# One step product of weighed halves in the wavefront scan, the logarithm in two pieces, and reworked edges between the stages of a conv-attention kernel

## The chip, the cores and the metric

The kernel runs on one core of one Trainium2 chip. The metric is device time in microseconds for one execution. The median of three runs of the kernel before is 4778.52 us (4757.96 to 4780.98).

## The reference, cut to what matters

The input is 64 images of 32 x 32 cells with 128 channels. Four layers follow one another: a scan, two attention layers, a scan. A scan visits all 1024 cells in a fixed spiral order and rewrites each from itself and its neighbours:

```python
def step(g, inp):                 # ci: the cell; ni, nm, nc: its neighbours, a mask, their number
    local = g[:, ci, :]
    neigh = (g[:, ni, :] * nm[None, :, None]).sum(axis=1) / nc
    u = jnp.concatenate([local, neigh], axis=-1)              # 256 channels
    y_sc = jnp.tanh(u @ w1 + b1) @ w2 + b2                    # 256 hidden values, one scalar a cell
    return (g.at[:, ci, :].set(local + y_sc[:, None] * w_y[None, :]), None)
# attention: q, k of 16 channels, v of 128; all 1024 cells of an image attend to all
attn = jax.nn.softmax(jnp.einsum('bnd,bmd->bnm', q, k), axis=-1)
out = gamma * jnp.einsum('bnm,bmc->bnc', attn, v) + inputs    # gamma in the first layer only
```

Everything is float32.

## The kernel before

**Scan.** Channels lie on the 128 partitions. Cells that don't depend on each other form a level; there are 122 levels with 16 cells at first and 1 at the end (509 cells stand in levels 0 to 35). A level's work is done for 32 images at once in two streams, A and B, up to level 63 (`JOIN` is 64), and from there for all 64 images in one stream. So an operand has 32 x 16 = 512 columns at level 0 and 32 x 11 = 352 at level 35. A product of the 256 hidden values is made in two halves of 128. For a stream and a level:

- POOL adds the neighbours that are not yet updated (`late_sums`, L562).
- DVE adds updated neighbours of older levels (L686) and those of the level just before (L688, together with `b2 * w_y`). The neighbours of the level just before are at that time without their step, so DVE adds the step of that level to the sums from PSUM when it is there (`add_steps`, L711). `EDGES` scales the sums of border cells (L695).
- PE makes `w1_own` times the cell (`own_products`, L906, 2 products), `w1_sum` times the sum (`near_products`, L916, 2 products); ACT takes the tanh of both halves (`squash`, L842).
- PE makes the step, w2[k] * w_y[c] times the hidden values, as 2 products that add up in PSUM (`steps`, L925). DVE adds it to the cells (`update`, L719).

Each engine works its queue in order. PE's order is, for each level, stream A (steps, own and near products of the next level), then B. DVE's is, for each level and stream: `add_steps` of the next level, `update` of this one, `sums` of the level after the next.

The cells live in `arena`, 512 places for each image, filled and emptied by chunks of levels. `load` (L411) and `store` (L417) move one chunk of one stream, as 4096 pieces of a few cells each; all are issued on SP, whose queue is in order too. `ENDING` is a chunk of 16 cells that are last in their ring; `first_loads` brings the chunks that have no earlier tenant of their places, for A, then for B.

**Attention.** 128 jobs (2 layers x 64 images, group A's 32 images through both layers, then B's). A job has 8 slices s on every engine; in a slice PE makes two key products (L954), a row product (L967), and the mix of probabilities and values: one full float32 product (L983) for the even block, and for the odd block three products of rounded parts (L988, L989, L991). The low part of the odd block is made by POOL (`split_probs`, L571) from what DVE rounded (L786). `row_maximum` (L748, DVE) and `row_sums` (L857, ACT) serve the softmax shift of the next job: POOL turns the sums into logarithms in one piece of 12 small instructions at s = 2 (`log_sums`, L582 to L605), between two `split_probs`. PE transposes the shift at s = 5 (`turn_shift`, L1034). `output` (L805, DVE) adds the mix to the image, SP stores it at s = 2 of the next job and loads a later one at s = 3 (`load_image`, L460), from the DRAM tensors `layer_out`.

**Edges.** The first job's image is loaded (L460) once all chunks of group A have been stored. `prepare_scan` weighs the scan weights on DVE, for the second scan after the first scan. 12 jobs before the end (`EARLY`), SP issues `first_loads` of the second scan for A, and after the last job those for B.

## Time and profile before

| | us |
|---|---|
| median of 3 runs | 4778.52 |
| lowest, highest | 4757.96, 4780.98 |
| the profiled execution | 4771.76 |
| its span, first to last instruction | 4769.6 |

| engine | busy us of the span | share |
|---|---|---|
| PE | 4486.8 | 94% |
| PE weight loads (beside the products) | 2312.6 | 48% |
| DVE | 3579.9 | 75% |
| ACT | 2850.4 | 60% |
| POOL | 2278.8 | 48% |

The profiled execution took 2.2 us more than its span. In the trace the first scan takes the time up to about 793 us, the attention jobs from 816 to 3997 us, the second scan the rest. In the timeline rows below, the first number is the start and the second the time taken by the instructions merged in the row; a count (x4) says how many records that is. A float32 product has two records on PE.

### The profile page before, as it was taken

The page shows a single profiled execution, that of the slowest core. Times are in us where ns is not written, and L with a number is a line of the kernel's source. Part 1 is how long each engine was busy: PE and PEld are TensorE (multiplying, and loading weights), DVE is VectorE, ACT ScalarE, POOL GpSimd, SP SyncE. Part 2 cuts the span into 40 slices and gives each one's busy share as a digit, 9 for nine tenths or more (in the row PEclk, how much of TensorE's full clock was granted, in tenths as well). Part 3 has the DMA queues.
Part 4 walks back from the last instruction along what each step waited for, and adds up shares of the span by engine and source line. Part 5 has one row for each costly group of instructions (what it writes and reads, how often), then busy time and mean ns, then how long its engine had stood idle before and what let it go on. Part 6 is the DMA issues. An engine that isn't in the chain of part 4 may idle for free.

```text
span 4769.6 us, 56934 instructions
## 1 busy us (share of the span) xinstructions
PE 4486.8 (94%) x17064; PEld 2312.6 (48%) x17064; DVE 3579.9 (75%) x6748; ACT 2850.4 (60%) x5225; POOL 2278.8 (48%) x3972
## 2 busy tenths in 40 slices
PE   5999996999999999999999999999999798999997
PEld 2456754444444444444444444444444343446754
DVE  3888876777777777777777777777777574888876
ACT  1223322777777777777777777777777574223322
POOL 3454431455555555555555555555555455454431
PEclk7999998899999999999999999999999899999998
DMA  9569415111111111111111111111111515379625
GB/s 155 54 74 127 91 31 56 48 57 57 57 57 57 52 53 55 57 57 56 57 57 57 53 54 54 55 57 57 57 57 57 108 53 96 36 75 127 86 53 45
DMA packets 496962, 309.85 MB, mean 65 GB/s; under 512 B 443408, under 2 KB 446736, under 8 KB 496656
## 3 DMA queue, kind: packets, MB, share of 16 engines
q1 hardware_dynamic: 496656, 306.21, 32.7%
q8 instruction: 138, 2.26, 0.2%
q14 instruction: 168, 1.38, 0.1%
HBM read 137.34 MB, written 135.27 MB: 57 GB/s over the span
## 4 chain that ended last, share of the span: by engine, by line
PE 69%; POOL 14%; DVE 6%; issue 6%; SPq 2%; DMA 1%; ACT 1%; DVEq 0%; POOLq 0%; ACTq 0%
PE psum L983 14%; PE psum L925 9%; PE psum L916 8%; PE psum L906 8%; PE psum L954 7%; POOL probs_low L571 7%; PE psum L991 4%; PE psum L967 4%; PE psum L989 3%; PE psum L988 3%; PE psum L1024 3%; PE psum L1002 3%; PE psum L1011 3%; SPq L411 1%; DVE shared L711 1%
## 5 line engine op out<-in xcount | busy, mean ns | idle before, releaser
L571 POOL TENSOR_TENSOR probs_low<-shared,probs_high 128x512 fp32r<-128x512 f32 x1024 | 1307.9, 1277 | 1387.9 <-DVE probs_high L786 1387.9
L748 DVE TENSOR_REDUCE top<-psum 128x1 f32<-128x1024 f32 x1024 | 1253.5, 1224 | 596.8 <-PE psum L967 596.6
L852 ACT ACTIVATE shared<-psum 128x512 f32<-128x512 f32 x2048 | 1108.9, 594 | 376.0 <-PE psum L954 375.8
L857 ACT ACTIVATE psum<-psum,top 128x1024 f32<-128x1024 f32 x1024 | 1114.3, 1088 | 311.0 <-DVE top L748 311.0
L983 PE MATMUL psum<-shared 128*128 128x512 f32 x2048 | 1127.4, 632 | 3.3 <-DVE x L805 0.7
L842 ACT ACTIVATE shared<-psum,b_col 128x320 f32<-128x320 f32 (+10 forms) x744 | 413.3, 566 | 1101.5 <-PE psum L916 1086.5
L562 POOL TENSOR_TENSOR shared<-arena 128x32 f32<-128x32 f32 (+6 forms) x1230 | 570.6, 494 | 870.4 <-PE psum L916 802.6
L988 PE MATMUL psum<-probs_high,v_high 128*128 128x512 f32 x1024 | 813.1, 794 | 0.0
L906 PE MATMUL psum<-arena,w_own 128*128 128x320 f32 (+12 forms) x1672 | 543.3, 453 | 42.2 <-DMA arena<-x_cells 38.3
L916 PE MATMUL psum<-shared,w_sum 128*128 128x320 f32 (+10 forms) x1488 | 529.4, 478 | 42.1 <-POOL shared L562 28.4
L786 DVE CAST probs_high<-shared 128x512 fp32r<-128x512 f32 x1024 | 538.8, 526 | 21.3 <-ACT shared L852 21.3
L925 PE MATMUL psum<-shared,w2wy 128*128 128x320 f32 (+10 forms) x1488 | 519.0, 471 | 13.8 <-ACT shared L842 7.1
L954 PE MATMUL psum<-q,k 64*128 64x512 f32 x2048 | 513.4, 497 | 0.3 <-ACT shared L852 0.3
L991 PE MATMUL psum<-probs_low,v_high 128*128 128x512 f32 x1024 | 419.6, 410 | 93.2 <-POOL probs_low L571 93.2
L983 PEld LDWEIGHTS psum<-shared 128*128 128x128 f32 x2048 | 306.3, 189 | 367.2 <-ACT shared L852 202.1
L967 PE MATMUL psum<-k,q 64*128 64x512 f32 x2048 | 411.2, 398 | 11.8 <-ACT psum L857 6.0
L906 PEld LDWEIGHTS psum<-arena,w_own 128*128 128x128 f32 x1672 | 306.6, 191 | 232.2 <-issue 138.9
L711 DVE SCALAR_TENSOR_TENSOR shared<-psum,shared 128x32 f32<-128x32 f32 (+10 forms) x954 | 294.1, 345 | 162.2 <-PE psum L925 152.3
L989 PE MATMUL psum<-probs_high,v_low 128*128 128x512 f32 x1024 | 401.8, 392 | 0.0
L916 PEld LDWEIGHTS psum<-shared,w_sum 128*128 128x128 f32 x1488 | 259.0, 191 | 257.7 <-DVE shared L711 123.5
L688 DVE SCALAR_TENSOR_TENSOR shared<-arena,b2wy,shared 128x256 f32<-128x256 f32 (+15 forms) x530 | 305.0, 576 | 100.9 <-POOL shared L562 82.2
L925 PEld LDWEIGHTS psum<-shared,w2wy 128*128 128x128 f32 x1488 | 264.1, 190 | 227.6 <-issue 103.6
(71 smaller groups left out, 4094.8 us busy)
## 6 DMA issues: line engine op xcount, KB each, us to landing
x<-layer_out SPq DMA_DIRECT2D x128, 512.0 KB, 3.2
layer_out<-x SPq DMA_DIRECT2D x128, 512.0 KB, 2.6
q<-q SPq DMA_DIRECT2D x256, 128.0 KB, 2.3
arena<-x_cells SPq DMA_DIRECT2D x8, 1520.0 KB, 10.4
layer_out<-arena SPq DMA_DIRECT2D x8, 1520.0 KB, 19.3
arena<-layer_out SPq DMA_DIRECT2D x8, 1520.0 KB, 10.7
y_cells<-arena SPq DMA_DIRECT2D x8, 1520.0 KB, 20.4
arena<-x_cells SPq DMA_DIRECT2D x4, 1504.0 KB, 18.8
```

Of the source, the lines that this page charges most:

```text
L571: nc.gpsimd.tensor_tensor(probs_low[n % 2][:], probs[u % PROBS], probs_high[n % 2][:], ALU.subtract).then_inc(probs_split, 1)
L748: nc.vector.reduce_max(top[i % 2][:, m:m + 1], rows_ps[m % 2][:], AX_X, negate=True).then_inc(row_max, 1)
L852: nc.scalar.activation(probs[u % PROBS], keys_ps[u % 2], ACT.Exp).then_inc(probs_ready, 1)
L857: nc.scalar.activation(rows_ps[m % 2][:], rows_ps[m % 2][:], ACT.Exp, bias=top[i % 2][:, m:m + 1], accum_out=total[i % 2][:, m:m + 1]).the ...
L906: nc.tensor.matmul(columns(pre(c, lv, h), c, lv, o, w), w1_own[n][:, tile(h)], arena[:, PICTURES[c], place:place + w], start=(m == 0), sto ...
L916: nc.tensor.matmul(columns(pre(c, lv, h), c, lv), w1_sum[n][:, tile(h)], cells(near[lv % 2], c, lv), start=False, stop=True, skip_group_ch ...
L925: mm = nc.tensor.matmul(columns(step(c, lv), c, lv), w2wy[n][h][:], cells(hidden[h], c, lv), start=(h == 0), stop=(h == HALVES - 1))
L954: nc.tensor.matmul(keys_ps[g], k[i % DEEP][ROW_GROUPS[g], tile(m)], q[i % 3][ROW_GROUPS[g], half(queries_at(g, h))], start=True, stop=True ...
L967: mm = nc.tensor.matmul(rows_ps[m % 2][:, half(g)], q[i % 3][ROW_GROUPS[g], tile(queries_at(g, h) * MT // 2 + r)], k[i % DEEP][ROW_GROUPS[ ...
L983: nc.tensor.matmul(mix_ps, v[i % 2][:, t], probs[u % PROBS], start=(m == 0), stop=False).then_inc(mixed, 1)
L988: nc.tensor.matmul(mix_ps, v_high[i % 2][:, t], probs_high[n % 2][:], start=False, stop=False)
L991: nc.tensor.matmul(mix_ps, v_high[i % 2][:, t], probs_low[n % 2][:], start=False, stop=(m == MT - 1)).then_inc(mixed, 1)
```

## The change

- **Levels 0 to 35** (`WEIGHED` = 36): DVE makes one operand `hidden0 + hidden1 * (w2_small / w2_big)` (`weigh`), and PE one step product with the weights of the first half. For the quotient to be at most 1 in size, the halves of w1, b1 and w2 are exchanged, hidden value by hidden value, so that the larger of the two w2 stands first (`larger_first`, 36 small DVE instructions for each scan).
- In these levels `add_steps` is gone. `update` comes first, and the sums over the level just before read the updated cells. PE's order becomes steps A, near B, own A of the next level, steps B, near A of the next level, own B of the next level; DVE's update A, new sums A, weigh B, old sums A of the level after, and the same for B.
- **Logarithm**: the polynomial is rearranged to 12 instructions in two pieces of 6, at s = 2 and s = 3, with one `split_probs` between them.
- **Chunks**: 14 instead of 13; the first are smaller (levels 0 to 1, 2 to 5, 6 to 7: 32, 64 and 31 cells), and the ending chunk takes in levels from 114 on (28 cells instead of 16). The last other chunk ends with level 113. The first loads are ordered by need: four chunks of A, four of B, the other four of A, of B.
- **Scan weights** are loaded on ACT's queue, and `prepare_scan(1)` with its `larger_first` is done by DVE in the midst of the first scan, at level 20.
- **Scan to attention**: the first 4 images are loaded except for their last 66 cells when the chunk before those is stored; ACT copies the 66 cells from `arena`.
- **Attention to scan**: no block of loads 12 jobs before the end. After each job of the second layer two loads put that image's first 511 cells of the second scan into `arena` (`refill`); ACT copies those of the very last image.

The diff, cut to its core:

```diff
-WINDOW = 5 * CHUNK - 16
+TAIL = 114
+WINDOW = 452
...
-    first = [0, 2]
-    for lv in range(2, LEVELS):
+    first = [0, 2, 6, 8]
+    for lv in range(8, TAIL):
...
+        def load_first_images():
+            for k in range(ENDING - 1):
+                sp.wait_ge(stored[A][k], 16)
+            sp.wait_ge(scan_weights_ready, 2 * (2 + HALVES))
+            for i in range(DEEP):
+                sp.dma_start(x[i][:, 0:OPEN], inner[0][i, :, 0:OPEN]).then_inc(x_in[i], 16)
+        def refill(i):
+            if is_job(i) and job_layer(i) == LAYERS - 1 and i < JOBS - 1:
+                g, b = i // (LAYERS * IMAGES), job_image(i)
+                sp.wait_ge(out_stored[i % DEEP], 16 * (i // DEEP + 1))
+                first = PLACES[0]
+                sp.dma_start(arena[:, b, first:first + KEPT], inner[LAYERS][b, :, 0:KEPT]).then_inc(refilled[g], 16)
+                sp.dma_start(arena[:, b, chunk_places_of(ENDING)], inner[LAYERS][b, :, chunk_cells(ENDING)]
+                             ).then_inc(refilled[g], 16)
...
-            load_scan_weights(0)
-            first_loads(0, A)
-            load_scan_weights(1)
-            first_loads(0, B)
+            for part in (FIRST_LOADS[:4], FIRST_LOADS[4:]):
+                for g in (A, B):
+                    for k in part:
+                        load(0, g, k)
...
                     if s == 6:
                         place_shift(j + 1)
+                        refill(j - 1)
...
-                if j == EARLY:
-                    first_loads(1, A)
...
-            first_loads(1, B)
...
             # log_sums(i), at s = 2
             nc.gpsimd.tensor_tensor(ratio[:], shrink[i % 2][:], total[i % 2][:], ALU.mult)
             nc.gpsimd.tensor_scalar(excess[:], ratio[:], -1.0, None, ALU.add)
+            nc.gpsimd.tensor_tensor(log_sum[:], top[i % 2][:], guess[i % 2][:], ALU.subtract)
             nc.gpsimd.tensor_tensor(square[:], excess[:], excess[:], ALU.mult)
+            nc.gpsimd.tensor_scalar(slope[:], excess[:], -0.25, 1.0 / 3.0, ALU.mult, ALU.add)
+            nc.gpsimd.tensor_tensor(slope[:], slope[:], excess[:], ALU.mult)
+        def shift_values(i):     # at s = 3
+            nc.gpsimd.tensor_scalar(slope[:], slope[:], -0.5, None, ALU.add)
+            nc.gpsimd.tensor_tensor(log_sum[:], log_sum[:], excess[:], ALU.subtract)
+            nc.gpsimd.tensor_tensor(slope[:], slope[:], square[:], ALU.mult)
+            nc.gpsimd.tensor_tensor(ratio[:], log_sum[:], slope[:], ALU.subtract)
             nc.gpsimd.tensor_copy(high, ratio[:])
             nc.gpsimd.tensor_tensor(low, ratio[:], high, ALU.subtract)
...
+        def weigh(n, c, lv):
+            dve.wait_ge(tanh_ready[c], levels_done(n, c, lv) * HALVES)
+            nc.vector.scalar_tensor_tensor(cells(hidden[0], c, lv), cells(hidden[1], c, lv), w2_ratio[n][:],
+                                           cells(hidden[0], c, lv), ALU.mult, ALU.add).then_inc(weighed[c], 1)
...
+            for lv in range(WEIGHED):
+                for c in (A, B):
+                    update(n, c, lv)
+                    new_sums(n, c, lv + 1)
+                    if c == A:
+                        weigh(n, B, lv)
+                    elif lv + 1 < WEIGHED:
+                        weigh(n, A, lv + 1)
+                    if lv + 2 <= WEIGHED:
+                        old_sums(n, c, lv + 2)
+                    else:
+                        sums(n, c, lv + 2)
+                if (n, lv) == (0, 20):
+                    prepare_scan(1)
...
         prepare_heads()
-        prepare_scan(1)
...
+        act.wait_ge(updated[BOTH], len(SPAN[BOTH]))
+        fill_first_images()      # 4 x 2 copies arena -> x
...
+        fill_last_picture()      # 2 copies x -> arena, after the last job
...
+            if lv < WEIGHED:
+                pe.wait_ge(weighed[c], n * WEIGHED + lv + 1)
+                nc.tensor.matmul(columns(step(c, lv), c, lv), w2wy[n][0][:], cells(hidden[0], c, lv),
+                                 start=True, stop=True).then_inc(step_ready[c], 1)
+                return
...
+            for lv in range(WEIGHED):
+                steps(n, A, lv)
+                near_products(n, B, lv)
+                own_products(n, A, lv + 1)
+                steps(n, B, lv)
+                near_products(n, A, lv + 1)
+                own_products(n, B, lv + 1)
```

## Rows read from the trace of the kernel before

**Rows 1.** Busy by stretch: PE, PEld, DVE, ACT, POOL; granted clock, DMA share, GB/s

```profile
66.00:395.00 329.00, 328.73 (x872) 159.84 (x873) 268.64 (x738) 90.49 (x140) 164.29 (x390) 0.99 0.62 78
820.00:3700.00 2880.00, 2778.10 (x11373) 1358.66 (x11373) 2188.89 (x2939) 2236.78 (x4113) 1503.98 (x2348) 0.99 0.17 55
```

**Rows 2.** Waits, 820 to 3990 us: total us, times, longest us

```profile
PE psum L991 <- POOL probs_low L571: 93.2, 127, 0.9
...
PE psum L1002 <- DMA x<-layer_out: 25.5, 1, 25.5
```

**Rows 3.** Timeline of PE and ACT about level 34, 352 columns

```profile
380.76 1.35 PE L916 MATMUL psum<-shared,w_sum 128*128 128x352 f32 x4
...
381.55 1.15 ACT L842 ACTIVATE shared<-psum,b_col 128x352 f32<-128x352 f32 x2 [2.51 <-PE psum L916]
...
381.94 1.35 PE L925 MATMUL psum<-shared,w2wy 128*128 128x352 f32 x4
```

**Rows 4.** Groups by form, 66 to 395 us: busy us, mean ns of one

```profile
L842 ACT ACTIVATE shared<-psum,b_col 128x512 f32<-128x512 f32 x30 | 20.6, 688 | 94.9 <-PE psum L916 94.9
...
L688 DVE SCALAR_TENSOR_TENSOR shared<-arena,b2wy,shared 128x352 f32<-128x352 f32 x13 | 7.7, 595 | 0.5
L688 DVE SCALAR_TENSOR_TENSOR shared<-arena,b2wy,shared 128x512 f32<-128x512 f32 x10 | 7.5, 752 | 0.4
...
L842 ACT ACTIVATE shared<-psum,b_col 128x352 f32<-128x352 f32 x10 | 5.5, 555 | 12.5 <-PE psum L916 12.3
```

**Rows 5.** DVE's group of added steps, 66 to 395 us

```profile
L711 DVE SCALAR_TENSOR_TENSOR shared<-psum,shared 128x32 f32<-128x32 f32 (+14 forms) x206 | 74.8, 395 | 40.3 <-PE psum L925 37.8
```

**Rows 6.** Timeline of one job about the logarithm

```profile
2013.39 0.20 POOL L582 TENSOR_TENSOR ratio<-shrink,total 128x8 f32<-128x8 f32 x1
...
2015.19 0.47 DVE L786 CAST probs_high<-shared 128x512 fp32r<-128x512 f32 x1
...
2016.78 1.28 POOL L571 TENSOR_TENSOR probs_low<-shared,probs_high 128x512 fp32r<-128x512 f32 x1
...
2018.11 0.50 PE L991 MATMUL psum<-probs_low,v_high 128*128 128x512 f32 x1 [0.53 <-POOL probs_low L571]
...
2019.20 0.23 PE L1034 MATMUL psum<-ident_r,shift 128*16 128x128 f32 x1
```

**Rows 7.** Timeline of the start; SPq is SP issuing DMAs

```profile
4.56 30.08 SPq L411 DMA_DIRECT2D arena<-x_cells  x7
...
43.97 31.33 SPq L411 DMA_DIRECT2D arena<-x_cells  x7
...
61.25 1.64 POOL L562 TENSOR_TENSOR shared<-arena 128x32 f32<-128x32 f32 x3 [35.96 <-DMA arena<-x_cells]
...
66.27 3.78 PE L916 MATMUL psum<-shared,w_sum 128*128 128x512 f32 x4 [8.47 <-POOL shared L562]
```

**Rows 8.** Timeline from the first scan to the first job

```profile
792.83 0.34 DVE L719 SCALAR_TENSOR_TENSOR arena<-psum,b2wy,arena 128x64 f32<-128x64 f32 x1 [2.27 <-PE psum L925]
...
795.64 0.29 DVE L626 TENSOR_SCALAR w_sum<-w_sum 128x256 f32<-128x256 f32 x1
...
816.11 1.97 PE L1002 MATMUL psum<-x,wk_rows 128*64 128x512 f32 x4 [23.31 <-DMA x<-layer_out]
```

**Rows 9.** SP's queue 12 jobs before the end

```profile
3711.21 28.57 SPq L411 DMA_DIRECT2D arena<-layer_out  x7
```

**Rows 10.** Timeline from the last job to the second scan

```profile
3996.63 1.66 POOL L562 TENSOR_TENSOR shared<-arena 128x32 f32<-128x32 f32 x3 [0.63 <-PE psum L991]
...
3998.36 3.25 POOL L562 TENSOR_TENSOR shared<-shared,arena 128x32 f32<-128x32 f32 x4
...
4019.42 3.78 PE L916 MATMUL psum<-shared,w_sum 128*128 128x512 f32 x4 [9.11 <-POOL shared L562]
```

**Rows 11.** Timeline of the end: SP's last stores, DVE's last update

```profile
4744.47 19.69 SPq L417 DMA_DIRECT2D y_cells<-arena  x4
...
4746.56 0.33 DVE L719 SCALAR_TENSOR_TENSOR arena<-psum,b2wy,arena 128x64 f32<-128x64 f32 x1 [2.12 <-PE psum L925]
```

More of the change, by code:

```diff
@@ L243, in turn_count @@
 def turn_count(n, c, lv):
[L245 removed]
+    per = [len(SUMS_OLD[v]) + len(SUMS_NEW[v]) + len(EDGES[v]) + (step_turns(c, v) if v > WEIGHED else 0)
+           for v in SPAN[c]]
     return n * sum(per) + sum(per[:lv - SPAN[c].start])
@@ L272, in first_chunks @@
     return [k for k in range(NC) if min(first_use[chunk_cells(k)]) == lv]
+FIRST_LOADS = sorted((k for k in range(NC) if not earlier_tenants(k)),
+                     key=lambda k: (min(FIRST_READ[chunk_cells(k)]), -chunk_size(k) if k else -CELLS))
+KEPT = sum(chunk_size(k) for k in FIRST_LOADS if k != ENDING)
+OPEN = STARTS[CHUNKS[ENDING - 1]]
 def is_job(i):
@@ L490, in place_shift @@
                                  shift_row[i % 2][:, cells_of]).then_inc(shift_placed[i % 2], 16)
-        def first_loads(n, g):
-            for k in (0, ENDING, *range(1, ENDING)):
-                if not earlier_tenants(k):
-                    load(n, g, k)
         def follow(n):
@@ L677, in sums, with new_sums @@
                         dve.wait_ge(updated[e], levels_done(n, e, lv - 2))
-            done = 0
-            for o, w, s0, s1 in (*SUMS_OLD[lv], *SUMS_NEW[lv]):
+            for m, (o, w, s0, s1) in enumerate(SUMS_OLD[lv]):
+                out = near[lv % 2][:, PICTURES[c], o:o + w]
+                if s0 is None and m > 0:
+                    dve.wait_ge(near_turn[c], turn_count(n, c, lv) + m)
+                in0 = out if s0 is None else arena[:, PICTURES[c], s0:s0 + w]
+                nc.vector.tensor_tensor(out, in0, arena[:, PICTURES[c], s1:s1 + w], ALU.add
+                                        ).then_inc(near_turn[c], 1)
+        def new_sums(n, c, lv):
+            if lv <= WEIGHED:
+                dve.wait_ge(updated[c], levels_done(n, c, lv - 1))
+            turn = turn_count(n, c, lv)
+            done = len(SUMS_OLD[lv])
+            for o, w, s0, s1 in SUMS_NEW[lv]:
                 out = near[lv % 2][:, PICTURES[c], o:o + w]
@@ L723, in scan @@
         def scan(n):
+            weigh(n, A, 0)
             for c in (A, B):
-                sums(n, c, 1)
-            for lv in range(JOIN - 1):
+                old_sums(n, c, 1)
+            for lv in range(WEIGHED):
[8 more added lines that the diff above has]
+                        old_sums(n, c, lv + 2)
+                    else:
+                        sums(n, c, lv + 2)
+                if (n, lv) == (0, 20):
+                    prepare_scan(1)
+            for lv in range(WEIGHED, JOIN - 1):
                 for c in (A, B):
@@ new lines, in load_weight_rows, with fill_first_images @@
+        def load_weight_rows(n):
+            act.dma_start(x[DEEP - 1][:, n * HID:(n + 1) * HID], scan_weights[n][2].rearrange("(a c) -> a c", a=1).to_broadcast([P, HID])
+                          ).then_inc(scan_weights_in[n], 16)
+        def fill_first_images():
+            for i in range(DEEP):
+                for k in (ENDING - 1, ENDING):
+                    nc.scalar.activation(x[i][:, chunk_cells(k)], arena[:, i, chunk_places_of(k)], ACT.Copy
+                                         ).then_inc(x_tail, 1)
@@ L883, in _ @@
+        with nc.allow_non_contiguous_dma(reason="rows to all partitions"):
+            load_scan_weights(0)
+            load_weight_rows(0)
+            load_scan_weights(1)
+            load_weight_rows(1)
+        act.wait_ge(scan_weights_in[0], 16 * 9)
         for lv in range(LEVELS):
```

182 lines of the change are left out of this document (132 added, 50 removed).

## The prediction

> **What bounds the kernel now.** I read the busy time by stretch first. Levels 0 to 35 of the first scan lie between 66 and 395 us, and there PE is busy 328.73 of 329 us at a clock of 0.99, while DVE has 268.64 and POOL 164.29 [rows 1]. The reader should see that PE alone sets this stage: a product less is time less, as long as nothing else comes up to it. In the attention jobs PE has 2778.10 of 2880 us, ACT 2236.78, DVE 2188.89. The waits say what the rest is: 93.2 us before L991, once in each job (127 times), for POOL's low parts, and one wait of 25.5 us for an image [rows 2]. The timelines of the start, of the two changes of stage and of the end then show stretches in which PE has nothing to do because data or sums are late [rows 7 to 11].
>
> **Step products of levels 0 to 35.** Two step products are issued 381.94 - 380.76 = 1.18 us after two near products of 352 columns began [rows 3], so a product of that width takes h = 0.59 us, and one of 512 columns 0.86 us. A half cycle (one stream, one level) has 6 products now: 5.15 us at 512 columns, 3.54 us at 352. It keeps 5: 4.29 and 2.95 us. The mean level has 509 / 36 = 14.1 cells, 452 columns, h = 0.76 us. There are 36 levels x 2 streams x 2 scans = 144 half cycles, so the bound of the gain is 144 x 0.76 = 109 us.
>
> Against it stands a longer chain. From a stream's steps A to the steps B that follow, PE makes steps A and near B, then ACT the second tanh of B, then DVE weighs, then PE may go on: 3 h + tanh + weighing + handovers. The first tanh began at 381.55 and both end at 382.70, so with 0.555 us for one the second began at 382.15, which is 0.20 us after two products' time from 380.76 [rows 3, 4]. It is also 0.04 us after the modelled end of the near products, and I take 0.04 for each of the other two handovers: 0.28 us in all. The weighing is an instruction like L688 (two operands in SBUF, one column of scalars): 0.752 us at 512 columns and 0.595 at 352; tanh is 0.688 and 0.555 [rows 4]. The chain is 2.57 + 0.69 + 0.75 + 0.28 = 4.29 us at 512 columns, as much as PE's 5 products, and 1.77 + 0.56 + 0.60 + 0.28 = 3.20 us at 352, more than 2.95. The gain is thus 0.86 us a half cycle at 512 and 0.34 at 352, and 0.34 + (100 / 160) x 0.52 = 0.66 at 452: 144 x 0.66 = 95 us.
>
> DVE must fit in. It loses the added steps, 74.8 us [rows 5], and gains 72 weighings of about 0.69 us, 50 us: 268.6 - 74.8 + 50 = 244 us for 72 half cycles, 3.4 us each, against 329 / 72 - 0.66 = 3.9 us. It has room, but at 87% in a fixed order it will now and then hold up a weighing. POOL's late sums take 164.29 / 72 = 2.3 us of a half cycle on the mean. For such meetings I take off 7 us: **88 us**, between 65 (0.2 us more on each half cycle) and 109.
>
> A rule of the Trainium skill speaks against this part. "SBUF — State Buffer", section "Who interferes with whom", says that a DVE instruction with two SBUF inputs and a GpSimd instruction that reads SBUF exclude each other for their whole length; the removed steps had one input in PSUM, the weighing has two in SBUF. L688 has two as well and ran at 0.752 us beside POOL, so the trace shows the rule cheap at most; what it could cost is the first rival below.
>
> **Logarithm.** The piece of 12 instructions runs from 2013.39 to 2016.78 us, 0.28 us each, and holds back L571, though what L571 reads was rounded by 2015.66. L571 then takes 1.28 us, and L991 starts at 2018.11 after a wait of 0.53 [rows 6]; the mean wait is 93.2 / 127 = 0.73 us. With 6 instructions first (1.70 us, to 2015.09) L571 can start at 2015.66 and is done at 2016.94, long before L991 would want it (2018.11 - 0.53 = 2017.58). The wait is gone. What is late next is the shift: the second piece runs from 2016.94 to 2018.64, and `turn_shift` (L1034), before at 2019.20, wants it at 2018.67, or up to 0.2 us sooner in jobs whose wait was 0.73. So 0.05 us a job may come back there. ACT (2236.78 / 2880, 18.8 us of a job of 24.2) and DVE are below PE's 23.5 us. 128 x (0.73 - 0.07) = **85 us**, between 40 (a part comes back at the shift or at ACT, which in slices without projections is about as full as PE) and 93.
>
> **The loads 12 jobs before the end.** SP issues 7 of them for 28.57 us [rows 9], the image's load stands behind them, and PE waits 25.5 us [rows 2]. The `refill` loads are two issues a job of 128 long pieces, at a place where SP has waited already for something later than they need. They come ahead of the swap of queries, which has slack. The whole wait goes, and with it some products at half clock after it: **27 us**, 25 to 28.
>
> **From the last job to the second scan.** POOL's sums for A take 3996.63 to 4001.61, 4.98 us. Those for B stood behind loads, and near B of level 0 began at 4019.42 [rows 10]. Now B's sums follow A's, to 4006.6, and near B starts at 4006.65: 12.8 us, and the one step product of A is already made, 0.9 us. ACT's two copies are ready at about 3997.6, before B's sums. Of the half clock after the old wait I count 1 us: **15 us**, 12 to 17.
>
> **From the first scan to the first job.** The first projection (L1002) began at 816.11. It now needs ACT's copies (after 793.2) and DVE's `prepare_heads`, done at 795.64 [rows 8]: 20.5 us sooner. But SP has two stores of the ending chunk to issue then, at 19.69 / 4 = 4.92 us each [rows 11], to 803; the swap of the first queries stands behind them and their data. I take off 4: **17 us**, 12 to 20.5.
>
> **The start.** A load takes 31.33 / 7 = 4.48 us of SP's queue; B's sums started at 61.25, 17.3 us after the first of B's three needed loads was issued [rows 7]. The third now has four loads of A and four places of weights less and more ahead of it: 0.7 + 4 x 4.48 + 17.3 = 35.9 us. That is 25 us sooner, and near B, 5.0 us after it, at 41 instead of 66.27. Then B's chunk of levels 8 to 13 is late: it is the 13th load, issued by 0.7 + 13 x 4.48 = 59 and landed some 3 to 10 us after, while DVE wants sums with it at about 41 + 2.5 x 8.6 = 62.5. 5 us come back: **20 us**, 12 to 25. DVE's `larger_first` and ACT's issues lie ahead of the sums and under the loads.
>
> **The end.** SP issued four stores from 4744.47, 4.92 us each, the last update being at 4746.56 [rows 11]. Two of them, of the chunk that now ends at level 113, are issued some 20 us before. The other two run from 4746.9 to 4756.7 instead of to 4764.16: **7 us**, 6 to 8.
>
> **What it costs.** `larger_first` and `prepare_scan(1)` are 40 DVE instructions in the midst of the scan, where DVE has little to spare. By the 0.29 us of L626 [rows 8] each is 11.6 us; the 18 small ones of `prepare_heads` took 2.5 us (793.1 to 795.6), 0.14 each, which makes 5.6. With both kinds, **8 us** lost. The chunk transfers must be done in a shorter scan, their DMA share being 0.62 on the mean [rows 1]; I count **4 us** of late loads in the two scans, 0 to 20.
>
> **The sum.** 88 + 85 + 27 + 15 + 17 + 20 + 7 - 8 - 4 = 247 us. The profiled execution took 4771.76 us, so 4525. It lay 6.8 us below the median; of three runs that scatter by 23 us I carry half of it: **4528 us**. The bounds of all terms together would be gains of 145 and 295 us.
>
> **Rivals.**
>
> - *The weighing and POOL block one another.* Each weighing waits out one of POOL's sums, 164.29 / 390 = 0.42 us [rows 1], instead of the 7 us counted: 144 x 0.42 = 60, 53 more: 4581 us. For it: both fall just behind the near products. Against it: L688 at 0.752 us. 0.14. By the rule of the Trainium skill above, this is what would happen if the two always met.
> - *The wait of the job moves instead of going.* The shift is ready too late for L1034, or ACT or DVE takes over, and of 85 us only 25 come: 4588 us. For it: 2018.64 against 2018.67. Against it: the delay at L1034 can't be more than a few tenths, and POOL's work is the same. 0.12.
> - *Chunks land late in the shorter scan.* 16 us for each scan: 4560 us. For it: loads issued at the last read of the chunk before. Against it: 0.62 share, and no such wait now after the start. 0.12.
> - *The streams stop covering each other* (the other side). If DVE's order lets one stream's update and new sums start only when the other's whole chain is done, a half cycle is the chain (3.8 us at 452 columns) plus update and new sums (2.1 us by three instructions of L688's kind): 5.9 instead of 4.6 us, a loss of 1.3 x 144 = 187 instead of a gain of 88: 4528 + 275 = 4803 us. It decides from 1.8 us on each half cycle. Against it: DVE takes 3.4 us of a half cycle, and update and new sums of one stream have the time of near, own and steps of the other. 0.02.
> - *My forecast*: 0.60, with 4490 to 4560 as its own range.
>
> Together: range 4485 to 4600 us. A measurement of this kernel can tell about 0.5% (24 us) from no change. Only the last rival is slower; within 0.5% nothing worked out above lies, and I leave 0.01 for it.
>
> **What would show it.** Near and step products: PE busy about 5/6 of before in the early levels, and its idle time before L925 small at 512 columns and about 0.25 us at 352. L991's wait near zero, some tenths at most before L1034. No PE gap about 3728 us of the old time, and none over 10 us at either change of stage. One DVE block of some 8 us at level 20 with PE idle. I would be wrong if PE's idle time before the steps grew to 0.5 us and more on each half cycle, or if the job's length stayed at 24.2 us instead of 23.5.

## The result and the profile after

The kernel after takes 4535.32 us (median of 4 runs, 4533.02 to 4536.9) against 4778.23 for the kernel before beside it (4 runs, 4757.96 to 4780.98): ratio 0.95, 95% interval 0.9474 to 0.9526, 243 us faster. The forecast was 4528, but part of that closeness is luck: the total hides terms that missed on both sides, so most of what follows takes the sum apart.

The first two parts of the page of the kernel after, shortened; its profiled execution took 4535.49 us:

```profile
span 4533.4 us, 56308 instructions
PE 4349.7 (96%) x16776; PEld 2252.3 (50%) x16776; DVE 3476.5 (77%) x6544; ACT 2842.2 (63%) x5235; POOL 2267.5 (50%) x3972
...
PE   6989996999999999999999999999999999999996
```

The line numbers have moved: `weigh` is L801, near products L1078 (before L916), own products L1068, the single step product L1087, `update` L825, POOL's late sums L588, the cast L907, `split_probs` L597, the third product L1166 (before L991), `turn_shift` L1211, the row product L1142, projections L1179, `load` L434, `store` L440.

**Stages.** PE, PEld, DVE, ACT and POOL by stretch, as in [rows 1]: the early levels and the jobs.

```profile
42.00:336.00 294.00, 273.20 (x680) 124.29 (x680) 255.40 (x600) 85.01 (x130) 163.49 (x367) 0.97 0.81 105
...
825.00:3750.00 2925.00, 2908.47 (x12130) 1444.85 (x12129) 2212.69 (x3128) 2369.15 (x4378) 1579.28 (x2505) 1.00 0.20 63
```

In the jobs PE has hardly a gap left (16.5 us of 2925, before 101.9 of 2880). In the early levels PE, which was busy 328.73 of 329 us, is now idle for 7%, 20.8 us, of which 7.6 lie at the block of level 20. Its 273.20 us are the 5/6 of before that the prediction named. DVE is busy for 0.87 of the time instead of 0.82. POOL's late sums are the same instructions as before, but from B's update of level 0 to that of level 35 of the first scan they take 179.0 us in all instead of 168.8.

**What PE waits for in the jobs**, 825 to 3750 us; these lines stand where L991's 93.2 us stood [rows 2]:

```profile
PEld psum L1211 <- POOL shift L633: 70.9, 125, 1.0
...
PEld psum L1166 <- POOL probs_low L597: 0.2, 1, 0.2
...
PE psum L1211 <- POOL shift L633: 0.2, 1, 0.2
```

The wait has moved to the weight load of `turn_shift`, 0.57 us a job, but weight loads run beside products: PE itself waits there 0.2 us in all. No image is waited for 12 jobs before the end either.

**Groups of the weighing and the late sums**, 42 to 336 us, with mean ns of one behind the busy time:

```profile
L801 DVE SCALAR_TENSOR_TENSOR shared<-shared,w_ratio 128x512 f32<-128x512 f32 x15 | 14.1, 942 | 0.8
L801 DVE SCALAR_TENSOR_TENSOR shared<-shared,w_ratio 128x448 f32<-128x448 f32 x16 | 13.6, 850 | 3.7 <-ACT shared L962 3.5
...
L588 POOL TENSOR_TENSOR shared<-arena 128x384 f32<-128x384 f32 x4 | 4.3, 1077 | 0.0
```

The weighing was costed by L688, 0.752 us at 512 columns [rows 4]. It takes 0.94.

**The start** answers to [rows 7]:

```profile
0.72 55.49 SPq L434 DMA_DIRECT2D arena<-x_cells  x12
...
37.43 1.67 POOL L588 TENSOR_TENSOR shared<-arena 128x32 f32<-128x32 f32 x3 [9.99 <-DMA arena<-x_cells]
...
42.49 3.78 PE L1078 MATMUL psum<-shared,w_sum 128*128 128x512 f32 x4 [8.32 <-POOL shared L588]
```

Near B begins 23.8 us sooner than at 66.27 (predicted 25), and later POOL waits once for a chunk (8.4 us, at 72.77), PE never waits for one. (The work of levels 1 to 8 is the same in both scans, and the first takes 75.9 us for it and the second 74.7, so this wait costs about 1.2 us.)

**From the first scan to the first job** answers to [rows 8]:

```profile
749.64 0.33 DVE L825 SCALAR_TENSOR_TENSOR arena<-psum,b2wy,arena 128x64 f32<-128x64 f32 x1 [1.91 <-PE psum L1092]
750.00 14.89 SPq L440 DMA_DIRECT2D layer_out<-arena  x2
...
752.47 1.97 PE L1179 MATMUL psum<-x,wk_rows 128*64 128x512 f32 x4 [2.87 <-DVE bk_rows L750]
...
764.93 28.71 SPq L504 DMA_DIRECT2D q<-q  x4
778.59 1.22 PE L1142 MATMUL psum<-k,q 64*128 64x512 f32 x4 [20.40 <-DMA q<-q]
```

The projection starts 2.5 us after the last update, where it waited 23.31 us before. But the row product behind it waits 20.40 us for the swap of queries, which SP issues only at 764.93, after two stores that hold its queue for 14.89 us. In that stretch the granted clock is at its lower level:

```profile
749.00:779.00 30.00, 4.95 (x13) 1.43 (x14) 5.63 (x23) 1.08 (x8) 0.00 (x0) 0.50 1.46 48
```

It stays at 0.5 until 816 us but for 3.4 us, and in the kernel before it was 0.50 from 788 to 859. So in both kernels the first products of the jobs run at half the clock.

**From the last job to the second scan**, with [rows 10]:

```profile
3797.38 1.67 POOL L588 TENSOR_TENSOR shared<-arena 128x32 f32<-128x32 f32 x3 [0.64 <-PE psum L1166]
...
3802.35 1.67 POOL L588 TENSOR_TENSOR shared<-arena 128x32 f32<-128x32 f32 x3
```

B's sums follow A's at once, as the prediction had it.

**The end.** The profile's groups of DMA issues after 4440 us; the last number is the time from issue to landing:

```profile
y_cells<-arena SPq DMA_DIRECT2D x2, 1520.0 KB, 22.8
y_cells<-arena SPq DMA_DIRECT2D x2, 608.0 KB, 24.4
y_cells<-arena SPq DMA_DIRECT2D x2, 448.0 KB, 24.5
```

The last update ends at 4504.59 and the span at 4533.4: 28.8 us. Before it was 22.7, with two more stores behind the last update. The end got 6 us longer, not 7 shorter.

### The profile page after: what moved, and what is told of

The parts are those of the page before. It is cut to its first block, busy times and chain, and to the rows that moved or that the text cites. A ratio compares the mean times of both kernels' runs of the same rounds, so it can differ in the third digit from the quotient of the medians.

```text
span 4533.4 us, 56308 instructions
## 1 busy us (share of the span) xinstructions
PE 4349.7 (96%) x16776; PEld 2252.3 (50%) x16776; DVE 3476.5 (77%) x6544; ACT 2842.2 (63%) x5235; POOL 2267.5 (50%) x3972
## 4 chain that ended last, share of the span: by engine, by line
PE 64%; DVE 9%; ACT 8%; issue 8%; POOL 7%; SPq 2%; DMA 0%; DVEq 0%; POOLq 0%; ACTq 0%
PE psum L1158 14%; PE psum L1078 7%; PE psum L1129 6%; PE psum L1068 6%; PE psum L1092 5%; POOL probs_low L597 4%; PE psum L1142 3%; PE psum L1166 3%; PE psum L1164 3%; PE psum L1163 3%; PE psum L1201 3%; PE psum L1179 3%; PE psum L1188 3%; ACT shared L972 3%; PE psum L1087 3%
## 5 line engine op out<-in xcount | busy, mean ns | idle before, releaser
L597 POOL TENSOR_TENSOR probs_low<-shared,probs_high 128x512 fp32r<-128x512 f32 x1024 | 1307.4, 1277 | 1300.2 <-DVE probs_high L907 1300.2
L588 POOL TENSOR_TENSOR shared<-arena 128x32 f32<-128x32 f32 (+6 forms) x1230 | 588.7, 509 | 764.8 <-PE psum L1078 725.2
L1068 PE MATMUL psum<-arena,w_own 128*128 128x320 f32 (+12 forms) x1672 | 539.5, 450 | 21.6 <-DVE w2wy L713 20.8
L1078 PE MATMUL psum<-shared,w_sum 128*128 128x320 f32 (+10 forms) x1488 | 523.3, 474 | 28.7 <-POOL shared L588 13.7
L907 DVE CAST probs_high<-shared 128x512 fp32r<-128x512 f32 x1024 | 427.2, 417 | 20.1 <-ACT shared L972 20.1
L1142 PE MATMUL psum<-k,q 64*128 64x512 f32 x2048 | 411.6, 398 | 28.3 <-DMA q<-q 21.1
L1068 PEld LDWEIGHTS psum<-arena,w_own 128*128 128x128 f32 x1672 | 305.8, 191 | 211.6 <-issue 127.0
L1166 PE MATMUL psum<-probs_low,v_high 128*128 128x512 f32 x1024 | 406.4, 397 | 0.0
L1078 PEld LDWEIGHTS psum<-shared,w_sum 128*128 128x128 f32 x1488 | 267.2, 190 | 235.3 <-issue 102.4
L1129 PEld LDWEIGHTS psum<-q,k 64*128 64x128 f32 x2048 | 191.1, 183 | 375.7 <-issue 374.5
L1163 PEld LDWEIGHTS psum<-probs_high,v_high 128*128 128x128 f32 x1024 | 194.7, 190 | 245.2 <-issue 244.7
L1164 PEld LDWEIGHTS psum<-probs_high,v_low 128*128 128x128 f32 x1024 | 194.6, 190 | 245.1 <-issue 245.1
L766 DVE TENSOR_TENSOR shared<-shared,arena 128x32 f32<-128x32 f32 (+7 forms) x832 | 278.0, 334 | 39.1 <-DVE shared L766 0.2
```

The lines of the kernel that those rows point to most:

```text
L588: nc.gpsimd.tensor_tensor(out, in0, arena[:, PICTURES[c], s1:s1 + w], ALU.add).then_inc(late_ready[c], 1)
L597: nc.gpsimd.tensor_tensor(probs_low[n % 2][:], probs[u % PROBS], probs_high[n % 2][:], ALU.subtract).then_inc(probs_split, 1)
L1068: nc.tensor.matmul(columns(pre(c, lv, h), c, lv, o, w), w1_own[n][:, tile(h)], arena[:, PICTURES[c], place:place + w], start=(m == 0), sto ...
L1078: nc.tensor.matmul(columns(pre(c, lv, h), c, lv), w1_sum[n][:, tile(h)], cells(near[lv % 2], c, lv), start=False, stop=True, skip_group_ch ...
L1129: nc.tensor.matmul(keys_ps[g], k[i % DEEP][ROW_GROUPS[g], tile(m)], q[i % 3][ROW_GROUPS[g], half(queries_at(g, h))], start=True, stop=True ...
L1142: mm = nc.tensor.matmul(rows_ps[m % 2][:, half(g)], q[i % 3][ROW_GROUPS[g], tile(queries_at(g, h) * MT // 2 + r)], k[i % DEEP][ROW_GROUPS[ ...
```

## The experiments

Durations of stages below are differences of the ends of DVE's updates, read from each profiled execution. Before, scan 1 needs 322.90 us from B's update of level 0 to that of level 35, and after 309.05; scan 2 324.08 and 298.07. The kernel before scatters by 33 us over all its runs (4748 to 4782), and its medians beside the kernel after and beside the three groups of experiments are 4778, 4778, 4752 and 4760; the changed kernels scatter by some 1 to 5 us. So a ratio of one group can't be set beside a ratio of another, and the changed kernels are compared with the 4535.3 of the kernel after, which was not measured again beside them. What supports this is that stages which an edit doesn't touch repeat: the jobs take 2971.6 to 2972.3 us in all ten kernels that have both the new logarithm and the new loads.

### The logarithm alone

The kernel before, with the 12 instructions rearranged as in the change; only their places are shown:

```diff
                 if s == 2:
                     log_sums(j + 1)          # 6 instructions
+                if s == 3:
+                    shift_values(j + 1)      # 6 instructions
```

> The kernel before with the logarithm in two pieces of 6 and nothing else changed. By the term of the prediction it is 85 us faster (4693), 0.66 us a job. If the idle time in the row understates the wait, because the matmuls in front overlap the one that waits when nothing holds it, it is 0.98 us a job: 125 us faster (4653). If the gain of the attention stage came from the other edits in it (refill, first images), only some 30 us are left (4748).

Measured: 4649.59 us (4648.48 to 4651.76) beside 4777.74, ratio 0.9731 (0.9715 to 0.9747), 128 us faster. The attention jobs, first to last output, went from 3123.8 to 3002.1 us: 121.7 us, 0.95 a job. Groups of DVE and PE in the jobs:

```profile
L790 DVE CAST probs_high<-shared 128x512 fp32r<-128x512 f32 x954 | 396.4, 416 | 0.6 <-ACT shared L856 0.6
...
L995 PE MATMUL psum<-probs_low,v_high 128*128 128x512 f32 x953 | 377.9, 397 | 0.0
```

The third product waits for nothing now. The row of 0.73 us a job [rows 2] was too small. In that trace the unhindered third product starts 0.23 us after the second, though the record of one is 0.40 long: the records of products overlap. The one after the logarithm:

```profile
2017.18 0.40 PE L989 MATMUL psum<-probs_high,v_low 128*128 128x512 f32 x1
2017.24 1.10 DVE L786 CAST probs_high<-shared 128x512 fp32r<-128x512 f32 x1
...
2018.11 0.19 PEld L991 LDWEIGHTS psum<-probs_low,v_high 128*128 128x128 f32 x1 [0.97 <-POOL probs_low L571]
2018.11 0.50 PE L991 MATMUL psum<-probs_low,v_high 128*128 128x512 f32 x1 [0.53 <-POOL probs_low L571]
```

These are of the kernel before. From start to start it is 0.93 us instead of 0.23, so 0.70 us are lost where the row says 0.53: the row counts from the modelled end of the product in front, 0.17 us after the next could have begun. 0.73 + 0.17 = 0.90 of the 0.95. The records bear it out: of the third products between 825 and 3680 us, 116 in the kernel before start more than 0.4 us after the second, at 1.13 us on the mean, which is 0.90 more than 0.23, and none does with the logarithm in two pieces. The last 0.05 stay open.

The same rows show something that the prediction had not priced, in the group of the cast in the kernel before, 825 to 3680 us:

```profile
L786 DVE CAST probs_high<-shared 128x512 fp32r<-128x512 f32 x926 | 487.7, 527 | 1.0 <-ACT shared L852 1.0
```

Its 0.527 us is a mean of two kinds. 810 of these casts take 0.417 us, and 116, once in each job, begin while the late `split_probs` of POOL runs and take 1.295. With two pieces three of 954 begin so and the mean is 0.416. What this is worth by itself was not tried.

### Without the weighing

```diff
-WEIGHED = 36
+WEIGHED = 0
...
-            weigh(n, A, 0)
             for c in (A, B):
-                old_sums(n, c, 1)
+                sums(n, c, 1)
...
+                if (n, lv) == (0, 20):
+                    prepare_scan(1)
```

The last two lines keep the block at level 20 in the loop that now has all levels.

> The kernel after with WEIGHED = 0: two step products in every level, add_steps as before, everything else kept. If the weighing gained the 88 us of the prediction, this takes 4623 us. If it gained the 48 us by which levels 0 to 35 became shorter in the trace, it takes 4583 us, and each scan's levels 0 to 35 are 22 to 26 us longer than in the kernel after.

Measured: 4592.8 us (4591.81 to 4594.57), ratio 0.9612 (0.9598 to 0.9627): the weighing is worth 57.5 us. In the two profiled executions, 59.1 us apart, 24.4 and 25.3 lie in levels 0 to 35 (333.49 and 323.35 us without it), and 5.9 and 4.9 in the first level of each scan, where B's update comes sooner; the rest is 1.4 us the other way. The run also isolates the rest: the jobs take 2972.3 us here, 29.8 less than with the logarithm alone, which is the block 12 jobs before the end.

### The tanh of the second half left in PSUM

```diff
-                nc.scalar.activation(cells(hidden[h], c, lv), columns(pre(c, lv, h), c, lv), ACT.Tanh,
+                out = columns(pre(c, lv, h), c, lv) if lv < WEIGHED and h == 1 else cells(hidden[h], c, lv)
+                nc.scalar.activation(out, columns(pre(c, lv, h), c, lv), ACT.Tanh,
...
-            nc.vector.scalar_tensor_tensor(cells(hidden[0], c, lv), cells(hidden[1], c, lv), w2_ratio[n][:],
+            nc.vector.scalar_tensor_tensor(cells(hidden[0], c, lv), columns(pre(c, lv, 1), c, lv), w2_ratio[n][:],
```

> The kernel after, with the tanh of the second half left in PSUM in levels 0 to 35, so that the weighing reads one operand from PSUM and one from SBUF. If the weighing is slow because POOL's sums and a DVE instruction with two SBUF operands keep each other out, its mean at 512 columns falls from 0.96 us to 0.75 or less and the two scans get 20 to 30 us shorter in all (4505 to 4515). If PE waits because the chain of steps, near products, tanh and weighing is as long as the 5 products of a half cycle, the weighing may get quicker but each scan stays within 5 us (4530 to 4540).

Measured: 4508.22 us (4507.24 to 4509.81), ratio 0.9435 (0.9421 to 0.9449), 27 us less than the kernel after. Levels 0 to 35 take 297.70 and 284.10 us, 11.4 and 14.0 less. The same groups and stretch as above:

```profile
L801 DVE SCALAR_TENSOR_TENSOR shared<-psum,w_ratio,shared 128x512 f32<-128x512 f32 x15 | 11.2, 748 | 1.9 <-ACT psum L963 1.4
L801 DVE SCALAR_TENSOR_TENSOR shared<-psum,w_ratio,shared 128x448 f32<-128x448 f32 x16 | 10.9, 684 | 2.8 <-ACT psum L963 2.2
...
L588 POOL TENSOR_TENSOR shared<-arena 128x384 f32<-128x384 f32 x4 | 3.3, 824 | 0.0
```

0.942 us has become 0.748, and POOL's 384-column sums fell from 1.08 to 0.82, though their instruction is the same. POOL's late sums of levels 1 to 35 take 151.2 us in all, 28 less than in the kernel after and also 18 less than in the kernel before, so they were held up before the change too. The same pair at level 2, first in the kernel after:

```profile
51.68 2.00 POOL L588 TENSOR_TENSOR shared<-arena 128x32 f32<-128x32 f32 x3 [1.84 <-PE psum L1078]
...
52.29 1.23 DVE L801 SCALAR_TENSOR_TENSOR shared<-shared,w_ratio 128x512 f32<-128x512 f32 x1
```

and with the half in PSUM:

```profile
52.52 1.62 POOL L588 TENSOR_TENSOR shared<-arena 128x32 f32<-128x32 f32 x3 [2.26 <-PE psum L1079]
...
53.10 0.75 DVE L801 SCALAR_TENSOR_TENSOR shared<-psum,w_ratio,shared 128x512 f32<-128x512 f32 x1
```

Both engines lose when they meet, 0.48 us on DVE and 0.38 on POOL here. This is the rival of the mutual block, and the runs show it at less than half the price it was given: 27 us at most, where it had 60. The edit also has ACT write the second tanh to PSUM, where it takes 0.662 us at 512 columns instead of 0.688; over 144 of them some 4 of the 27 us may be that (an estimate from these two rows). The first scan gains less than the second because POOL's wait for a chunk now reaches PE, which idles for 2.71 us at 79.01 and then has the half clock for 3.4: levels 1 to 8 take 75.5 us there and 71.0 in the second scan. The Trainium skill ("SBUF — State Buffer", section "Who interferes with whom") names this pair, and says that one input from elsewhere avoids it; both agree with the two traces.

### The second scan's weights prepared at the start

```diff
         prepare_scan(0)
+        prepare_scan(1)
         scan(0)
...
-                if (n, lv) == (0, 20):
-                    prepare_scan(1)
```

> The kernel after with prepare_scan(1) done right after prepare_scan(0), while DVE waits for the first chunks, instead of at level 20. If the block at level 20 costs what the level's step from 9.0 to 16.6 us says, the first scan is 7.6 us shorter (4528) and the start is not later. If the ops at the start hold up the first own sums or the first updates, the gain is lost in the first level (4535 or up to 5 us more).

Measured: 4524.81 us (4522.81 to 4526.04), ratio 0.9469 (0.9455 to 0.9483), 10.5 us less. The start is 1.0 us later and the levels 0 to 35 10.4 us shorter (298.66). In the kernel after, the block stands here:

```profile
233.49 0.28 DVE L660 TENSOR_SCALAR x<-x 128x256 f32<-128x256 f32 x1
...
241.15 0.48 DVE L713 TENSOR_SCALAR w2wy<-w2wy,w_col 128x128 f32<-128x128 f32 x2
...
244.31 1.83 PE L1087 MATMUL psum<-shared,w2wy 128*128 128x448 f32 x2 [7.62 <-DVE shared L801]
```

The 8.1 us of it cost 10.4. PE idles for 7.62 us, the granted clock falls to 0.5 from 239.2 to 249.5 us, and the two records of the product behind it take 1.83 us instead of 0.99 at the full clock. In the run with the early weights there is no such fall in these levels.

### The swap of queries ahead of the last stores

```diff
+        def store_ending():
+            for g in range(GROUPS):
+                store(0, g, ENDING)
...
+                if (n, what, k) == (0, "store", ENDING):
+                    continue
...
                         swap_queries(j + 3)
+                        if j == -3:
+                            store_ending()
```

> The kernel after, with the two stores of the ending chunk of the first scan issued on SP behind the first swap of queries. If the first job waits for the swap because it stands behind these stores, first output after the scan is 12 to 18 us sooner (4517 to 4523). If it waits for something else (the data of the image, POOL, the DMA engines still busy with the store before), the time stays within 3 us of 4535.

Measured: 4519.69 us (4517.45 to 4521.74), ratio 0.9512 (0.9497 to 0.9526) beside 4752.4, 15.6 us less than the kernel after. From the last update to the first output it takes 61.7 us instead of 76.0:

```profile
760.46 1.16 SPq L504 DMA_DIRECT2D q<-q  x2
761.67 3.54 SPq L440 DMA_DIRECT2D layer_out<-arena  x2
763.54 1.22 PE L1150 MATMUL psum<-k,q 64*128 64x512 f32 x4 [4.76 <-DMA q<-q]
```

The wait fell from 20.40 to 4.76 us, which is the 15.6 us. The same stores now cost SP 3.54 us and not 14.89. In the kernel after they are issued from 750.00, while the pieces of the stores in front of them run until 757.5; here they are issued at 761.67, when none of those is left. That an issue is held up by what the queue still has to move is the likely reason; it was not tested by itself.

### Where the ending chunk starts

A row of the DRAM tensor has 1024 cells of 4 bytes, and a store writes one piece of a chunk's cells for each row. Three runs move the boundary. The first puts the ending chunk back to 16 cells:

```diff
-TAIL = 114
+TAIL = 122
```

> The kernel after with TAIL = 122: the ending chunk is 16 cells from cell 1008 on (64-byte pieces that start on a 64-byte step of a DRAM row), the one before has 50 cells (200 bytes, ends on such a step). Four stores stand at the end again, as in the kernel before. If the price of the last stores is in pieces that neither start nor end on such steps (59 to 80 ns each against 22 to 39), the end is 6 us shorter than in the kernel after (22.7 instead of 28.8 us from the last update), 4529, though two stores more are issued after the last update. By the prediction's count of issues it is 7 us longer (4542).

The second and the third keep one arrangement of smaller chunks and differ by one level:

```diff
-CHUNK = 96
-TAIL = 114
-WINDOW = 452
+CHUNK = 90
+TAIL = 112        # third run: 113
+WINDOW = 448      # third run: 450
```

> The kernel after with TAIL = 112, the ending chunk being 32 cells from cell 992 on (128-byte pieces, starting on a 128-byte step), and chunks of up to 90 cells, so that the one before has 86. If unaligned ends of pieces are the price, the two last stores land within 12 us of their issue instead of 21 to 28, and the end from the last update is 14 to 20 us instead of 28.8 (4520 to 4527). If the price is by bytes or by pieces alone, the end stays at 27 to 30 us (4533 to 4540).

> The run with the ending chunk from cell 992, with the boundary moved by one level: the ending chunk is 30 cells from cell 994 (120-byte pieces, start 8 bytes off a 16-byte and 64-byte step), the one before 88 cells that end there. If the ends of pieces that lie off a 64-byte step are the price, a piece takes 50 ns and more on the mean instead of 17, the last stores land 20 to 30 us after the last update, and the time is 20 to 40 us more than with 992 (4505 to 4525). If the number of bytes, or the other chunk sizes, made that run fast, the time stays within 5 us of it (4482 to 4492).

Measured, with the time from the last update to the end of the span, and the mean time of one piece of the stores by the trace's records of the DMA:

```
last chunk from cell     kernel     us (lowest, highest)           ratio (95%)              end us
996  (112-byte pieces)   after      4535.32 (4533.02, 4536.9)      0.95   (0.9474, 0.9526)  28.8
1008 (64)                tail_1008  4526.61 (4526.25, 4528.3)      0.9527 (0.9513, 0.9541)  23.5
992  (128)               tail_992   4486.64 (4484.24, 4487.11)     0.9441 (0.9425, 0.9456)   8.0
994  (120)               tail_994   4519.23 (4518.76, 4520.84)     0.9497 (0.9482, 0.9513)  24.5

piece, cells, bytes      ends off a 32-byte step   mean ns of one
992 to 1024, 128         0                         17
1008 to 1024, 64         0                         17 to 24
994 to 1024, 120         1                         57
996 to 1024, 112         1                         59
958 to 1008, 200         1                         39 to 45
906 to 992, 344          1                         44 to 50
906 to 994, 352          2                         68
958 to 996, 152          2                         79

stores amid the scans, from the same records
672 to 768, 384          0                         22 to 26
383 to 472, 356          1                         35 to 38
472 to 558, 344          1                         40 to 43
558 to 645, 348          2                         71 to 84
```

The landing times of the last stores, issued together, with 992:

```profile
y_cells<-arena SPq DMA_DIRECT2D x2, 1376.0 KB, 17.9
y_cells<-arena SPq DMA_DIRECT2D x2, 512.0 KB, 5.8
```

and with 994:

```profile
y_cells<-arena SPq DMA_DIRECT2D x2, 1408.0 KB, 23.5
y_cells<-arena SPq DMA_DIRECT2D x2, 480.0 KB, 20.0
```

128 bytes a piece in 5.8 us, 120 bytes in 20.0: neither bytes nor pieces set the price, but the ends of the pieces. The expectations speak of a 64-byte step. The traces say that 32 bytes are enough: cell 472 (byte 1888 of its row) is a boundary in the runs with chunks of 90, 32 bytes past a 64-byte step, and the two chunks that meet there take 35 to 43 ns a piece, like others with one odd end, where chunks of 324 to 360 bytes with both ends odd take 57 to 84. Cell 996, 16 bytes past a step, does pay. It is not the length either: the 352 bytes from 906 to 994 are 11 times 32 and take 68. And it is the store alone that pays: the same 352-byte pieces are loaded at 22 ns. Of the 49 us by which 992 is faster than the kernel after, 20.8 lie at the end of the kernel and 17 between first scan and first output (58.9 us instead of 76.0: the stores ahead of the swap are short). 10 more lie in levels 36 to 121 of the scans (385.87 and 385.12 us against 390.32 and 390.64), and the third run keeps these (385.02 and 386.29), so they come with the smaller chunks and their places and not with the last boundary. The same instructions are a little shorter there; what in the cells' places does that was not tried. The third run gives back 16.5 us of the end and 16.5 of the way to the first output with the same chunk sizes but for two cells.

### All of it together

The kernel after with PSUM, early weights, swap first and the chunk from 992:

> The kernel after with the four edits that made it shorter: tanh of the second half left in PSUM, prepare_scan(1) at the start, stores of the ending chunk behind the first swap, ending chunk from cell 992. If they add up (26 + 10 + 49, the swap being without a wait in the last one already): 4450, 4445 to 4455. If the early levels hit another bound together, or the swap brings the stores onto the loads of the first images, 4460 to 4475.

Measured: 4452.52 us (4452.19 to 4453.11), ratio 0.9357 (0.9343 to 0.9371). Three of the four add up to within 4 us (27, 10.5 and 48.7 make 4449). The fourth, the swap ahead of the stores, gains nothing beside them: from the last update to the first output it takes 61.3 us, and with the chunk from 992 alone 58.9, since the short stores no longer hold up the swap. PE in the early levels:

```profile
42.00:336.00 294.00, 289.67 (x744) 134.52 (x743) 245.06 (x613) 89.18 (x142) 144.41 (x390) 0.99 0.99 123
```

PE is at 98.5% again. The DMA share is 0.99 on the mean, after 0.62 before the change; that is no ceiling, since the kernel after shows 1.46 in the row of 749 to 779 us. And with one step product up to level 59:

```diff
-WEIGHED = 36
+WEIGHED = 60
```

> The run with the four edits, and WEIGHED = 60 instead of 36, so that levels 36 to 59 have one step product too. By the chain of the prediction at 320 columns (a half cycle is 3.05 us with 6 products, so 0.51 us a product): 3 x 0.51 + 0.52 + 0.56 + 0.28 = 2.89 us, 0.16 less, times 96 half cycles = 15 us faster than that run. If DVE's order is what sets these levels (levels 31 to 35 were 0.09 us longer a half cycle with the weighing from SBUF than without, and 0.12 shorter with the one from PSUM), it is between 10 us faster and 10 us slower.

Measured: 4437.46 us (4434.55 to 4439.11), ratio 0.9324 (0.9311 to 0.9338), 15 us less, as its chain says. It is the fastest of all, 98 us below the kernel after.

## Why the prediction was right, and where it was not

| term | predicted us | measured us | by |
|---|---|---|---|
| step products | 88 | 57 | without the weighing |
| logarithm | 85 | 122 | logarithm alone, its jobs |
| block 12 jobs before the end | 27 | 30 | jobs, that run against the one without weighing |
| first scan to first job | 17 | 4 | last update to first output |
| last job to second scan | 15 | 12.5 | without the weighing |
| start | 20 | 23 | without the weighing |
| end | 7 | -6 | last update to end |
| the block at level 20 | -8 | -10 | moved to the start |
| late chunks | -4 | 0 | levels 36 to 121 |

The measured column gives 232 of the 236 us by which the span became shorter. That the forecast of 247 lies so near is luck in part: +37 of the logarithm stood against -31, -13 and -13 of the step products, the first job and the end. Two small sums of the prediction are off as well: its chances add up to 1.01, and the lower ends of its terms make a gain of 140 us, not 145.

- **Step products.** The mechanism was right, and the term was mis-sized in two places. The first is "for such meetings I take off 7 us": they cost 27 at most, so 20 more. The second is the chain behind the 95 us. With the weighing out of POOL's way the gain is 57.5 + 27 = 84.6 us, 10 short of it. In the second scan a half cycle then gains 0.80 us in levels 1 to 8 over the run without weighing (predicted 0.86 at 512 columns), 0.42 in levels 25 to 31 (416 columns, 0.55 by the prediction's line) and 0.12 in levels 32 to 35 (0.34 at 352). Which link of the chain is longer at narrow widths is open. The argument that "L688 has two as well and ran at 0.752 us beside POOL" was the mistake behind the 7 us. By the records of both engines, L688's 10 instructions at 512 columns each began ahead of POOL's. Of its 93 from 320 columns up, 42 began behind one of POOL's, at 0.03 us more on the mean, but with one of 1.28 us at 480 columns, where 0.72 is usual. Of the weighing's 72 it is 68, at 0.16 us more (0.22 at 512), since it comes just behind the near products, which release POOL's sums too. Those 0.16 x 144 are 23 of the 27 us, and the shorter tanh can be the rest. Why L688, when it came second, mostly paid nothing is open. In the last weighed levels the change as made is not even a gain: levels 32 to 35 take 29.57 us after and 28.83 without weighing, but 27.88 with the half in PSUM.
- **Logarithm.** The mechanism was right: no wait before the third product, a wait of POOL's shift in its place that costs next to nothing. The term was mis-sized, 0.66 us a job against 0.95. The idle time in the row is short by the overlap of two products (0.17 us), and I took 0.07 off for a return at the shift, which fell on the weight load. The rival "the wait moves" is out.
- **Block, start, second scan.** Within 3 us each. "B's chunk of levels 8 to 13 is late" came true for POOL alone, which waits 8.4 us for it and has the time: PE doesn't wait, and of the 5 us taken off for it 1.2 were there. The second scan's first level gained 5 us more through the weighing.
- **First scan to first job.** The projection came as predicted. "I take off 4" for the swap behind SP's stores failed: the issues held SP 14.9 us, not 9.8, and the swap then waited for its own pieces behind theirs (issued at 764.93, there at 778.59). Each part of it was named; its size was read from the mean time of an issue elsewhere. The run with the swap first gives 15.6 us of it back.
- **End.** "4.92 us each" made the number of stores the price. The price lay in the new chunk boundary, which this change itself moved from a 32-byte step (cell 1008) to 16 bytes past one (cell 996): with 1008 again, four stores end 5.3 us sooner than two do with 996. The cost of the pieces was read from stores of another shape, and the diff's `TAIL = 114` was read as a change of count alone.
- **The block at level 20** cost a little more than its own length. **Late chunks** were not there after the start; the rival is out, as is that of the streams that stop covering each other.

What stays open beside this: why levels 36 to 121 are 5 us shorter a scan with the other chunk places, and why the kernel before scatters more than those after it.

## What to carry to other kernels

Cost a new instruction by one that comes at the same place of the cycle, behind the same neighbours, not by one of its kind elsewhere: the weighing took 0.75 us alone and 1.23 behind POOL's sums. When a product waits, read the loss from start to start, since the idle time in the rows leaves out the overlap. And when a tensor is cut into pieces for DMA, put the cuts of what is written, the last above all, on steps of 32 bytes: one level's shift of a cut was worth 33 us here.

## What the runs showed of the hardware

- In stores of small pieces to DRAM, ends off a 32-byte step cost time: 57 ns a piece of 120 bytes with one such end against 17 for 128 with none. Over the scans' stores in all runs, pieces of 64 to 384 bytes take 11 to 28 ns with no odd end, 22 to 62 with one and 57 to 84 with two. The Trainium skill ("DMA: Bandwidth & Descriptors", section "Specifications") puts a read-modify-write at every transfer below 512 bytes; here pieces of 64 and 128 bytes show no such price, and 344 bytes with one odd end pay it. That it is a read-modify-write at the odd ends was not shown.
- SP's time to issue a store is not a property of the store: the same pair took 14.89 us behind stores that were still moving and 3.54 us when those were done.
- In this kernel a DVE instruction with two SBUF inputs that began while a sum of POOL ran took longer, and so did POOL's sums: the weighing by 0.2 us on the mean at 512 columns and by 0.66 at worst. One input in PSUM removes it at no price of its own (0.748 us against the 0.752 of the form in [rows 4]), and none of the 144 weighings is then held up.
- A cast on DVE with one SBUF input is held up too: 1.295 us behind POOL's `split_probs` against 0.417 otherwise.
